# Inverse norms of queries and keys: one power on GpSimd in place of eleven VectorE instructions

## The chip, the cores and the metric

The kernel runs on one core of one Trainium2 chip. Its time is the device time of one execution in microseconds (us). The cores' engines are TensorE (PE in the profile; its weight loads are PEld), VectorE (DVE), ScalarE (ACT), GpSimd (POOL) and SyncE (SP, which here only issues transfers). Each engine runs its own instruction list in order, and the engines meet through semaphores.

## The reference, cut to what matters

The input is x of 4 x 1024 tokens with 128 channels, in float32. A linear attention with a layer norm comes first, and then six layers, each of a windowed attention and a feed-forward part. The change lies in the windowed attention:

```python
def l2norm(t):
    return t / jnp.maximum(jnp.linalg.norm(t, axis=-1, keepdims=True), 1e-12)

q = l2norm(q) * qs
k = l2norm(k) * ksc
...
sim = jnp.einsum('bhwie,bhwje->bhwij', bq, bk2) * QK_SCALE
sim = jnp.where(mask, -jnp.finfo(sim.dtype).max, sim)
attn = jax.nn.softmax(sim, -1)
```

There are 16 heads of 64 channels, so each token has 16 query norms and 16 key norms. What is wanted of each is the inverse square root of a sum of 64 squares, held above 1e-24.

## The kernel before, in words

Tokens lie on the 128 partitions, so 4096 tokens are 32 tiles, and six layers make 192 tiles of windowed attention. After the 32 tiles of a layer comes its feed-forward part in eight groups of four tiles. Every engine has a hand-written order of its own for one step, which works on several tiles at once, each in another stage of its way (the argument `s` of each helper is how many tiles back it works). `schedule` runs the steps two at a time in a loop. No planner orders anything: what an engine does next is the next line of its step. One period of this loop is one tile.

One tile goes through the engines like this. ScalarE copies the transposed tokens out of PSUM and makes their rounded upper part `xsT_hi`. VectorE subtracts to get the lower part `xsT_lo` (L974). TensorE projects the queries (L539 to L541, three products for each half). ScalarE squares them (L1351). VectorE multiplies the projection by the cosine and the sine table (`rotate`, L995), which frees the PSUM banks; TensorE then projects the keys into the same banks. VectorE sums the squares of queries and of keys per head (`sum_of_squares`, L1007) into `sumsq`, 128x32. GpSimd adds the two rotated parts (`add_rotated`, L1570 and L1571) into `qk_rot`.

The inverse norms come from `sumsq` by eleven VectorE instructions on 128x32: a clamp (L1022), a seed made on the bit pattern (L733), and three Newton rounds of three instructions (L737, L738, L739), each waiting for the one before through the semaphore `norm_step`. They are spread over VectorE's step: the calls `inverse_norms(i0, i1, s)` at L1069 to L1080 and L1100 to L1104 put one or two of them between other instructions. The result `rnorm` has three readers. GpSimd multiplies the rotated keys by it (`normalise_k`, L1580), and `k_rotated` then lets TensorE transpose them (L553). VectorE multiplies the row maxima of the scores by it (`softmax_bias`, L1058, to `nbias`). ScalarE takes it as the scale of the exponentials (L1365). VectorE also makes the reciprocals of the row sums (L984, `rrow`), by which GpSimd scales the probabilities (`normalise`, L1557).

GpSimd's step is: `normalise_k(1)`, `normalise(0, 2)`, `normalise(1, 2)`, `add_rotated("q", 0)`, `add_rotated("k", 0)`. TensorE's step starts with the transposes of the first half of the keys of two tiles back, and then the key projection of one tile back.

The functions that the change touches, and what calls them:

Of the kernel before, what the change touches and what calls it, by code (L numbers as in the profile page):

```python
# [54 lines left out]
RSQRT_OPS = 11  # L55
# [44 lines left out]
def build(nc, consts, at, x, Wq, bq, Wk, bk, Wv, bv, Wo, bo, Wqkv, q_scale, k_scale, Wout,  # L100
          ln_g, ln_b, W1, b1, W2, b2, out):
    ctx = ExitStack()
    with ctx:  # L103
# [3 lines left out]
        def sem(name):  # L107
            return ctx.enter_context(nc.semaphore(name))
# [55 lines left out]
        rs_t = sb("rs_t", [P, 2 * H])  # L164
        rs_h = sb("rs_h", [P, 2 * H])
# [80 lines left out]
        norm_step = sem("norm_step")  # L246
# [476 lines left out]
        def _(dve):  # L723
            v = nc.vector

            def rsqrt(y, src, t, h, first, steps, base):

                ops = [
                    first,
                    lambda: v.tensor_scalar(y.bitcast(I32), src.bitcast(I32), -0.5, RSQRT_MAGIC, ALU.mult, ALU.add),  # L733
                ]
                for _ in range(3):
                    ops += [
                        lambda: v.tensor_tensor(t, y, y, ALU.mult),  # L737
                        lambda: v.scalar_tensor_tensor(h, t, -0.5, src, ALU.mult, ALU.mult),  # L738
                        lambda: v.scalar_tensor_tensor(y, h, 1.5, y, ALU.add, ALU.mult),  # L739
                    ]  # L740
                assert len(ops) == RSQRT_OPS

                def op(i):
                    if i:
                        dve.wait_ge(steps, base + i)
                    ops[i]().then_inc(steps, 1)
                return op


# [159 lines left out]
            with dve.Fori(0, DEPTH) as l:  # L909
# [26 lines left out]
                def step(k, par, it):  # L936
# [65 lines left out]
                    def sum_of_squares(qk, s):  # L1002
                        if not there(k, it, s):
                            return
                        T, n = T0 - s, "qk".index(qk)
                        dve.wait_ge(squared[qk], done(T))
                        v.tensor_reduce(sumsq[:, n * H:(n + 1) * H],  # L1007
                                        heads(squares[:, n * INNER:(n + 1) * INNER]), AX,
                                        ALU.add).then_inc(summed[qk], 1)

                    def inverse_norms(i0, i1, s):

                        if not there(k, it, s):
                            return
                        T, a = T0 - s, (par - s) % 2
                        if i0 == 0:
                            dve.wait_ge(summed["q"], done(T))
                            dve.wait_ge(summed["k"], done(T))
                        if i0 <= 1 < i1:
                            dve.wait_ge(k_rotated, done(T - 2))  # L1020
                        op = rsqrt(rnorm[:, a, :], sumsq[:, :], rs_t[:, :], rs_h[:, :],
                                   lambda: v.tensor_scalar(sumsq[:, :], sumsq[:, :], 1e-24, None, ALU.max),  # L1022
                                   norm_step, RSQRT_OPS * T)
                        for i in range(i0, i1):
                            op(i)
# [24 lines left out]
                    def softmax_bias(half, s):  # L1050

                        if not there(k, it, s):
                            return
                        T, a, h = T0 - s, (par - s) % 2, slice(8 * half, 8 * half + 8)
                        dve.wait_ge(exp_done[half], done(T - 1))
                        dve.wait_ge(norm_step, RSQRT_OPS * T + RSQRT_OPS)
                        dve.wait_ge(max_done[half], done(T))
                        v.scalar_tensor_tensor(nbias[:, h], smax[:, h], -1.0, rnorm[:, a, h], ALU.mult,  # L1058
                                               ALU.mult).then_inc(bias_ready[half], 1)
# [9 lines left out]
                    inverse_norms(3, 4, 1)  # L1069
                    if it is not None or k != 1:  # L1070
                        xsT_lower(0)
                    inverse_norms(4, 5, 1)
                    maxima(1, 2)
                    inverse_norms(5, 6, 1)
                    residual(3)
                    inverse_norms(6, 8, 1)
                    softmax_bias(1, 2)
                    inverse_norms(8, 9, 1)
                    row_reciprocals(0, 2)
                    inverse_norms(9, 11, 1)  # L1080
# [17 lines left out]
                    sum_of_squares("k", 0)  # L1098
                    maxima(0, 1)
                    inverse_norms(0, 1, 0)  # L1100
                    softmax_bias(0, 1)
                    inverse_norms(1, 2, 0)
                    rotate("k", 0, 0)
                    inverse_norms(2, 3, 0)  # L1104
# [365 lines left out]
        def _(pool):  # L1470
            g = nc.gpsimd

            g.memset(x_tok[:, :], 0.0).then_inc(zeroed, 1)
# [71 lines left out]
            with pool.Fori(0, DEPTH) as l:  # L1545
                def step(k, par, it):
# [25 lines left out]

                    def normalise_k(s):
                        if not there(k, it, s):
                            return
                        T, a = T0 - s, (par - s) % 2
                        pool.wait_ge(added["k"], done(T))
                        pool.wait_ge(norm_step, RSQRT_OPS * T + RSQRT_OPS)
                        kk = heads(qk_rot[:, 1, :])
                        g.tensor_tensor(kk, kk, rnorm[:, a, H:2 * H].unsqueeze(2).broadcast_to([P, H, D]),  # L1580
                                        ALU.mult).then_inc(k_rotated, 1)

                    normalise_k(1)
# [185 lines left out]
```

## Time and profile before

| | |
|---|---|
| median of 3 runs | 4097.17 us (4088.42 to 4102.23) |
| profiled execution, span | 4091.2 us; its own time outside the span is not listed apart |
| PE busy | 3424.9 us (84%) |
| PEld busy | 2264.8 us (55%) |
| DVE busy | 3354.0 us (82%) |
| ACT busy | 3114.5 us (76%) |
| POOL busy | 2097.8 us (51%) |
| granted TensorE clock, mean | 0.931 |

The span goes from the first to the last instruction of the profiled execution. Busy shares are means over stages: in the 32 tiles of a layer's attention the engines are busier than in its feed-forward part. A timeline row gives start, duration, engine, line, what is written from what, and in brackets the idle time just before it with what ended it. Rows on one engine may overlap by about 0.1 us, since the end of one instruction lies beside the start of the next.

### The profile page before, as it was taken

Reading aid. Unit: us, or ns where it says so; the run is one execution under the profiler, and the core shown is the slowest. Engines: PE = TensorE matmul, PEld = TensorE weight load, DVE = VectorE, ACT = ScalarE, POOL = GpSimd, SP = SyncE. Lnnn points to the kernel's source line nnn. Section 1 sums busy time; section 2 is a strip of 40 time slices with the busy share of each in tenths; the row PEclk is TensorE's granted clock in tenths of the full one; section 3 lists DMA queues with packets and bytes.
Section 4 is the critical chain, followed back from the end, with each engine's and each line's share of the span. In section 5 each row is a group of like instructions: output and inputs, shape, how many; then the busy total and the mean of one; then the engine's idle time right before and its main releaser. Section 6 shows DMA issues by size and latency. Waiting matters only on the chain. (4 is left out here: it accounts for less than half of the span.)

```text
span 4091.2 us, 121860 instructions
## 1 busy us (share of the span) xinstructions
PE 3424.9 (84%) x40924; PEld 2264.8 (55%) x40924; DVE 3354.0 (82%) x6043; ACT 3114.5 (76%) x9641; POOL 2097.8 (51%) x2534
## 2 busy tenths in 40 slices
PE   5688987788989679988688888877899867988977
PEld 4455555655555555555465555555555545555555
DVE  7798997489999569999659989856899966999975
ACT  3488897378998459988638888846889954998883
POOL 3455554455555345555445555534555544555544
PEclk8799998899999889999889999988999988999998
DMA  2000000100000100000100000010000010000001
GB/s 61 10 4 4 4 4 25 27 6 4 4 4 3 43 12 4 4 4 4 31 21 5 4 4 4 2 43 11 4 4 4 4 36 17 4 4 4 4 24 42
DMA packets 109598, 51.94 MB, mean 13 GB/s; under 512 B 62726, under 2 KB 106628, under 8 KB 108420
## 3 DMA queue, kind: packets, MB, share of 16 engines
q1 hardware_dynamic: 109444, 49.99, 4.9%
q8 instruction: 84, 1.38, 0.1%
q14 instruction: 70, 0.57, 0.0%
HBM read 22.57 MB, written 2.10 MB: 6 GB/s over the span
## 5 line engine op out<-in xcount | busy, mean ns | idle before, releaser
L1365 ACT ACTIVATE probs<-s_ps,nbias,rnorm 128x64 f32<-128x64 f32 x3072 | 1209.2, 412 | 92.3 <-DVE nbias L1058 82.7
L1570 POOL TENSOR_TENSOR qk_rot<-by_cos,by_sin 128x512 f32<-128x512 f32 x384 | 487.7, 1270 | 629.1 <-DVE by_sin L995 629.1
L604 PE MATMUL ring<-wvo,xsT 128*32 128x512 f32 x6144 | 776.5, 625 | 1.5 <-ACT qT L1173 1.0
L1557 POOL TENSOR_TENSOR probs<-probs,rrow 128x256 f32<-128x256 f32 x768 | 454.5, 613 | 565.7 <-DVE rrow L984 565.7
L1365 ACT ACTIVATION_READ_ACCUMULATOR probs<-s_ps,nbias,rnorm 128x1 f32 x3072 | 649.5, 211 | 0.0
L539 PE MATMUL qk_ps<-wqk_hi,xsT_hi 128*128 128x512 f32 x756 | 342.9, 454 | 333.8 <-DVE xsT_lo L974 333.8
L1351 ACT ACTIVATE squares<-qk_ps 128x1024 f32<-128x1024 f32 x378 | 386.1, 1021 | 222.6 <-PE qk_ps L541 222.0
L1580 POOL TENSOR_TENSOR qk_rot<-qk_rot,rnorm 128x1024 f32<-128x1024 f32 x192 | 365.3, 1902 | 361.6 <-DVE rnorm L739 361.6
L1007 DVE TENSOR_REDUCE sumsq<-squares 128x16 f32<-128x1024 f32 x384 | 464.0, 1210 | 82.8 <-ACT squares L1351 82.8
L553 PEld LDWEIGHTS ring<-cst,qk_rot 128*128 128x128 f32 x3072 | 372.1, 147 | 286.1 <-issue 216.9
L995 DVE TENSOR_TENSOR by_cos<-qk_ps,rotary 128x1024 f32<-128x1024 f32 x378 | 460.5, 1218 | 84.4 <-ACT squares L1351 54.0
L553 PE MATMUL ring<-cst,qk_rot 128*128 128x128 f32 x3072 | 478.8, 289 | 44.8 <-POOL qk_rot L1580 33.4
L1571 POOL TENSOR_TENSOR qk_rot<-by_cos,by_sin 128x512 f32<-128x512 f32 x384 | 502.3, 1308 | 0.0
L995 DVE TENSOR_TENSOR by_sin<-qk_ps,rotary 128x1024 f32<-128x1024 f32 x378 | 458.5, 1213 | 0.0
L590 PE MATMUL s_ps<-kT,qT 128*32 128x128 f32 x12288 | 415.6, 276 | 0.0
L622 PE MATMUL ring<-vo,pT 128*32 128x128 f32 x12288 | 384.6, 278 | 5.0 <-ACT pT L1173 5.0
L539 PEld LDWEIGHTS qk_ps<-wqk_hi,xsT_hi 128*128 128x128 f32 x756 | 148.7, 197 | 422.0 <-issue 334.1
L590 PEld LDWEIGHTS s_ps<-kT,qT 128*32 128x32 f32 x12288 | 312.5, 110 | 121.1 <-issue 121.1
L1173 ACT ACTIVATE kT<-ring 64x512 f32<-64x512 f32 x576 | 340.3, 591 | 40.4 <-PE ring L553 33.5
L1173 ACT ACTIVATE vo<-ring 128x512 f32<-128x512 f32 x576 | 332.3, 608 | 34.5 <-PE ring L604 33.7
L604 PEld LDWEIGHTS ring<-wvo,xsT 128*32 128x32 f32 x6144 | 169.2, 114 | 333.2 <-issue 302.5
L622 PEld LDWEIGHTS ring<-vo,pT 128*32 128x32 f32 x12288 | 333.6, 112 | 28.3 <-issue 7.3
(166 smaller groups left out, 6427.7 us busy)
## 6 DMA issues: line engine op xcount, KB each, us to landing
xs<-x_tok SPq DMA_DIRECT2D x194, 64.0 KB, 1.9
qk_rot<-L_ffn_Wqkv SPq DMA_DIRECT2D x7, 1024.0 KB, 6.5
by_cos<-x_tok SPq DMA_DIRECT2D x48, 128.0 KB
by_cos<-x_tok SPq DMA_DIRECT2D x48, 127.0 KB
wv<-L_ffn_Wqkv SPq DMA_DIRECT2D x7, 512.0 KB, 8.4
wo_pad<-L_ffn_Wo SPq DMA_DIRECT2D x14, 256.0 KB, 7.7
x_keep<-L_attn_x SPq DMA_DIRECT2D x4, 512.0 KB, 4.9
out<-x_keep SPq DMA_DIRECT2D x4, 512.0 KB, 4.5
```

The costliest lines, as they stand in the source:

```text
L539: mm(half, xsT_hi[:, a, :], wqk_hi[:, cols], start=True, stop=False)
L553: last = nc.tensor.transpose(r[:, p * P:(p + 1) * P], qk_rot[:, 1 if qk == "k" else 0, c:c + P], ident)
L590: last = mm(s_ps[WIN * w:WIN * (w + 1), half, p * P:(p + 1) * P], qT[:, 4 * half + p, WIN * w:WIN * (w + 1)], kT[:, 4 * half + p, :, c:c + ...
L604: last = mm(r[WIN * mh:WIN * (mh + 1), :], xsT[:, a, WIN * w:WIN * (w + 1)], wvo[:, mh, :, :], start=True, stop=True)
L622: last = mm(r[WIN * w:WIN * (w + 1), 0:C], pT[:, quad, side, WIN * w:WIN * (w + 1)], vo[:, at_w, quad * C:(quad + 1) * C], start=(n == 0), ...
L995: last = v.tensor_tensor(heads((by_sin if part else by_cos)[:, n, :]), heads(projection_banks(qk, k, it, s)), rotary[2 * n + part][:, bass ...
L1007: v.tensor_reduce(sumsq[:, n * H:(n + 1) * H], heads(squares[:, n * INNER:(n + 1) * INNER]), AX, ALU.add).then_inc(summed[qk], 1)
L1173: return nc.scalar.activation(out_, in_, ACT.Copy)
L1365: last = nc.scalar.activation(probs[:, a, h // 4, :, h % 4, :], s_ps[:, half, c:c + 2 * WIN].rearrange("p (s c) -> p s c", s=2), ACT.Exp, ...
L1557: last = g.tensor_tensor(p, p, r, ALU.mult)
L1570: g.tensor_tensor(d[:, :, lo], cs[:, :, lo], sn[:, :, hi], ALU.add)
L1571: g.tensor_tensor(d[:, :, hi], cs[:, :, hi], sn[:, :, lo], ALU.add).then_inc(added[qk], 1)
```

## The change

`minus_half` is a column of -0.5, written once by GpSimd at the start. VectorE keeps the clamp, in one place, after the sum of the keys' squares. The seed and the three Newton rounds go. GpSimd raises `sumsq` to the power -0.5 in one instruction at the head of its step, ahead of `normalise_k`. `clamped` and `rnormed` take the place of `norm_step`. As before, the new writer of `rnorm` waits until the keys of two tiles back are normalised, and now it waits also until their exponentials are done; `sum_of_squares` waits until the power of the tile before has read `sumsq`.

```diff
         def _(dve):
-            def rsqrt(y, src, t, h, first, steps, base):
-                ops = [
-                    first,
-                    lambda: v.tensor_scalar(y.bitcast(I32), src.bitcast(I32), -0.5, RSQRT_MAGIC, ALU.mult, ALU.add),
-                ]
-                for _ in range(3):
-                    ops += [
-                        lambda: v.tensor_tensor(t, y, y, ALU.mult),
-                        lambda: v.scalar_tensor_tensor(h, t, -0.5, src, ALU.mult, ALU.mult),
-                        lambda: v.scalar_tensor_tensor(y, h, 1.5, y, ALU.add, ALU.mult),
-                    ]
...
                         T, n = T0 - s, "qk".index(qk)
+                        dve.wait_ge(rnormed, done(T - 1))
                         dve.wait_ge(squared[qk], done(T))
...
+                    def clamped_squares(s):
+                        if not there(k, it, s):
+                            return
+                        T = T0 - s
+                        dve.wait_ge(summed["q"], done(T))
+                        dve.wait_ge(summed["k"], done(T))
+                        v.tensor_scalar(sumsq[:, :], sumsq[:, :], 1e-24, None, ALU.max).then_inc(clamped, 1)
...
                         dve.wait_ge(exp_done[half], done(T - 1))
-                        dve.wait_ge(norm_step, RSQRT_OPS * T + RSQRT_OPS)
+                        dve.wait_ge(rnormed, done(T))
...
-                    inverse_norms(3, 4, 1)
                     if it is not None or k != 1:
                         xsT_lower(0)
-                    inverse_norms(4, 5, 1)
                     maxima(1, 2)
-                    inverse_norms(5, 6, 1)
                     residual(3)
-                    inverse_norms(6, 8, 1)
                     softmax_bias(1, 2)
-                    inverse_norms(8, 9, 1)
                     row_reciprocals(0, 2)
-                    inverse_norms(9, 11, 1)
                     rotate("q", 0, 0)
...
                     sum_of_squares("k", 0)
+                    clamped_squares(0)
                     maxima(0, 1)
-                    inverse_norms(0, 1, 0)
                     softmax_bias(0, 1)
-                    inverse_norms(1, 2, 0)
                     rotate("k", 0, 0)
-                    inverse_norms(2, 3, 0)
                     rotate("k", 1, 0)
...
+            g.memset(minus_half[:, :], -0.5)
             g.memset(x_tok[:, :], 0.0).then_inc(zeroed, 1)
...
+                    def inverse_norms(s):
+                        if not there(k, it, s):
+                            return
+                        T, a = T0 - s, (par - s) % 2
+                        for half in range(2):
+                            pool.wait_ge(exp_done[half], done(T - 2))
+                        pool.wait_ge(k_rotated, done(T - 2))
+                        pool.wait_ge(clamped, done(T))
+                        g.tensor_tensor(rnorm[:, a, :], sumsq[:, :], minus_half[:, :].broadcast_to([P, 2 * H]),
+                                        ALU.pow).then_inc(rnormed, 1)
...
                         pool.wait_ge(added["k"], done(T))
-                        pool.wait_ge(norm_step, RSQRT_OPS * T + RSQRT_OPS)
+                        pool.wait_ge(rnormed, done(T))
...
+                    inverse_norms(1)
                     normalise_k(1)
```

## Rows read from the trace of the kernel before

**Rows 1.** The page's first lines: span, and each engine's busy time.
```profile
span 4091.2 us, 121860 instructions
PE 3424.9 (84%) x40924; PEld 2264.8 (55%) x40924; DVE 3354.0 (82%) x6043; ACT 3114.5 (76%) x9641; POOL 2097.8 (51%) x2534
```

**Rows 2.** Busy time by window: stretch, length, PE, PEld, DVE, ACT, POOL, clock, DMA share.
```profile
407.50:424.00 16.50, 14.43 (x195) 9.35 (x191) 15.51 (x28) 14.44 (x49) 9.24 (x10) 0.94 0.01 4
424.00:441.50 17.50, 15.79 (x211) 9.57 (x207) 14.98 (x27) 15.08 (x49) 9.20 (x9) 0.96 0.01 4
```

**Rows 3.** VectorE's timeline, 403 to 421 us: start, duration, instruction, idle before.
```profile
403.05 1.16 DVE L974 TENSOR_TENSOR xsT_lo<-xsT,xsT_hi 128x128 fp32r<-128x128 f32 x1 [0.32 <-ACT xsT_hi L1173]
404.12 1.27 DVE L739 SCALAR_TENSOR_TENSOR rnorm<-rs_h,rnorm 128x32 f32<-128x32 f32 x1
...
407.62 1.22 DVE L995 TENSOR_TENSOR by_cos<-qk_ps,rotary 128x1024 f32<-128x1024 f32 x1 [0.24 <-issue]
...
412.82 0.18 DVE L984 RECIPROCAL rrow<-psum_row 128x8 f32<-128x8 f32 x1
...
415.46 1.31 DVE L1058 SCALAR_TENSOR_TENSOR nbias<-smax,rnorm 128x8 f32<-128x8 f32 x1
416.69 0.17 DVE L733 TENSOR_SCALAR rnorm<-sumsq 128x32 int32<-128x32 int32 x1
416.77 1.21 DVE L995 TENSOR_TENSOR by_cos<-qk_ps,rotary 128x1024 f32<-128x1024 f32 x1
417.91 0.18 DVE L737 TENSOR_TENSOR rs_t<-rnorm 128x32 f32<-128x32 f32 x1
418.01 1.21 DVE L995 TENSOR_TENSOR by_sin<-qk_ps,rotary 128x1024 f32<-128x1024 f32 x1
...
419.72 1.07 DVE L974 TENSOR_TENSOR xsT_lo<-xsT,xsT_hi 128x128 fp32r<-128x128 f32 x1 [0.40 <-ACT xsT_hi L1173]
```

**Rows 4.** GpSimd's timeline over the same stretch.
```profile
404.01 1.33 POOL L1571 TENSOR_TENSOR qk_rot<-by_cos,by_sin 128x512 f32<-128x512 f32 x1
407.47 1.90 POOL L1580 TENSOR_TENSOR qk_rot<-qk_rot,rnorm 128x1024 f32<-128x1024 f32 x1 [2.12 <-DVE rnorm L739]
...
413.09 1.18 POOL L1557 TENSOR_TENSOR probs<-probs,rrow 128x256 f32<-128x256 f32 x2 [2.58 <-DVE rrow L984]
...
415.47 1.27 POOL L1571 TENSOR_TENSOR qk_rot<-by_cos,by_sin 128x512 f32<-128x512 f32 x1
419.39 1.25 POOL L1570 TENSOR_TENSOR qk_rot<-by_cos,by_sin 128x512 f32<-128x512 f32 x1 [2.65 <-DVE by_sin L995]
```

**Rows 5.** ScalarE's timeline over the same stretch.
```profile
406.03 1.02 ACT L1351 ACTIVATE squares<-qk_ps 128x1024 f32<-128x1024 f32 x1 [0.92 <-PE qk_ps L541]
...
419.31 0.31 ACT L1173 ACTIVATE xsT_hi<-xsT 128x128 fp32r<-128x128 f32 x1
```

**Rows 6.** TensorE's timeline: second half of query, first half of key transposes.
```profile
409.01 1.13 PE L553 MATMUL ring<-cst,qk_rot 128*128 128x128 f32 x8
```

**Rows 7.** VectorE's timeline in a tile with a shorter period.
```profile
1186.67 0.15 DVE L1058 SCALAR_TENSOR_TENSOR nbias<-smax,rnorm 128x8 f32<-128x8 f32 x1
...
1194.68 1.23 DVE L995 TENSOR_TENSOR by_cos<-qk_ps,rotary 128x1024 f32<-128x1024 f32 x1 [0.24 <-issue]
```

**Rows 8.** ScalarE's timeline in the same tile.
```profile
1192.55 1.02 ACT L1351 ACTIVATE squares<-qk_ps 128x1024 f32<-128x1024 f32 x1
```

**Rows 9.** Waits over the whole span: total us, times, longest us.
```profile
PE ring L553 <- POOL qk_rot L1580: 33.4, 37, 4.0
DVE by_cos L995 <- issue: 30.4, 129, 0.2
```

**Rows 10.** Groups by line: count, busy us, mean ns, idle before and releaser.
```profile
L739 DVE SCALAR_TENSOR_TENSOR rnorm<-rs_h,rnorm 128x32 f32<-128x32 f32 x576 | 304.9, 529 | 13.5
L1580 POOL TENSOR_TENSOR qk_rot<-qk_rot,rnorm 128x1024 f32<-128x1024 f32 x192 | 365.3, 1902 | 361.6 <-DVE rnorm L739 361.6
L1480 POOL TENSOR_TENSOR ln_rs<-ln_rs 128x4 f32<-128x4 f32 x156 | 30.5, 198 | 276.2 <-DVE ln_rs L766 269.1
```

More of the change, by code:

```diff
@@ L54 @@
 RSQRT_MAGIC = 1597463007.0
-RSQRT_OPS = 11
 NEWTON_OPS = 12
@@ L163, in build @@
         sumsq = sb("sumsq", [P, 2 * H])
-        rs_t = sb("rs_t", [P, 2 * H])
-        rs_h = sb("rs_h", [P, 2 * H])
+        minus_half = sb("minus_half", [P, 1])
         rnorm = sb("rnorm", [P, 2, 2 * H])
@@ L245, in build @@
             {qk: tile_sem(f"{qk}_{n}") for qk in "qk"} for n in ("projected", "squared", "summed", "read", "added")]
-        norm_step = sem("norm_step")
+        clamped, rnormed = tile_sem("clamped"), tile_sem("rnormed")
         k_rotated = tile_sem("k_rotated")
@@ L724, in _ @@
             v = nc.vector
-            def rsqrt(y, src, t, h, first, steps, base):
-                ops = [
-                    first,
-                    lambda: v.tensor_scalar(y.bitcast(I32), src.bitcast(I32), -0.5, RSQRT_MAGIC, ALU.mult, ALU.add),
-                ]
-                for _ in range(3):
-                    ops += [
-                        lambda: v.tensor_tensor(t, y, y, ALU.mult),
-                        lambda: v.scalar_tensor_tensor(h, t, -0.5, src, ALU.mult, ALU.mult),
-                        lambda: v.scalar_tensor_tensor(y, h, 1.5, y, ALU.add, ALU.mult),
-                    ]
[L741 to L747, printed above, removed]
             def wide(ap):
@@ L1009, in sum_of_squares @@
                                         ALU.add).then_inc(summed[qk], 1)
-                    def inverse_norms(i0, i1, s):
+                    def clamped_squares(s):
                         if not there(k, it, s):
                             return
[L1015 to L1025, printed above, removed]
+                        T = T0 - s
+                        dve.wait_ge(summed["q"], done(T))
+                        dve.wait_ge(summed["k"], done(T))
+                        v.tensor_scalar(sumsq[:, :], sumsq[:, :], 1e-24, None, ALU.max).then_inc(clamped, 1)
                     def carry(s):
```

## The prediction

> **What bounds the kernel now.** I read the page's busy line first, then the busy time by window over single tiles of the attention, then the four timelines side by side, and last the list of waits. The page shows four engines between 51% and 84% over a span of 4091.2 us [rows 1], so no engine is the bound by its share alone. Inside a tile the picture is tighter: in a period of 16.5 us VectorE works 15.5, TensorE and ScalarE 14.4, GpSimd 9.2; in the next period of 17.5 us TensorE works 15.8 and VectorE 15.0 [rows 2]. Idle time is left on every engine, so a loop of dependences sets the period, not a queue that is full. The timelines show the loop, here from one start of `rotate("q")` to the next:
>
> - VectorE from the cosine product of the queries at 407.62 to the reciprocals `rrow` at 412.82: 5.2 us [rows 3].
> - GpSimd scales the probabilities from 413.09 and adds the rotated queries until 416.74 [rows 4]. VectorE's `nbias` (L1058), which reads two SBUF tensors, is recorded from 415.46 for 1.31 us and ends just behind that instruction of GpSimd [rows 3, 4]: 3.95 us from the reciprocals.
> - ScalarE makes four exponentials and then `xsT_hi`, done at 419.62 [rows 5]: 2.85 us.
> - VectorE makes `xsT_lo`, from 419.72 to 420.79. It ends behind GpSimd's first addition of the keys, 419.39 to 420.64 [rows 3, 4]: 1.17 us.
> - TensorE projects the queries and ScalarE squares them: from the end of `xsT_lo` at 404.21 to the end of the square at 407.05 are 2.84 us [rows 3, 5], and the next cosine product follows 0.57 us later.
>
> These are 5.2 + 3.95 + 2.85 + 1.17 + 2.84 + 0.57 = 16.6 us, the period. Beside it TensorE has a path of its own: after the query projection it goes on without a pause to the first key transposes, done at 410.14 [rows 6], and projects the keys.
>
> **The change, part by part.** The sum is made on the span, 4091.2 us, which lies 6.0 us under the median of the runs, 4097.2; the time outside the span stays.
>
> *Removed between the two parts of `rotate("k")`.* The seed moves the cosine product from 416.69 to 416.77 and the first Newton instruction the sine product from 417.91 to 418.01 [rows 3]: 0.18 us. The sine product releases GpSimd's addition of the keys, and the end of that addition's first part releases `xsT_lo`. So 0.18 us comes off the loop in each tile: 192 x 0.18 = 35 us.
>
> *Removed between `xsT_lo` and `rotate("q")`.* Eight Newton instructions go. One of them (L739, from 404.12) is held for 1.27 us behind GpSimd's second addition, which ends at 405.34 [rows 3, 4]; that is why L739 has a mean of 529 ns over 576 instructions [rows 10]. VectorE reaches the cosine product late in 129 tiles, those where the releaser is "issue" and not the square [rows 9]. Where the square is the releaser the start follows it by 0.26 us (I take this lag for all), so 407.62 could be 407.31: 0.31 us. In the tile with the shorter period the square ends at 1193.57 [rows 8] and the product starts at 1194.68 [rows 7] and not at 1193.83: 0.85 us. By the gaps between `xsT_lo` and the product about 80 of the 129 are of the first kind and 49 of the second: 80 x 0.31 + 49 x 0.85 = 66 us. The other tiles gain nothing here.
>
> *Not removed.* The held `nbias` of the first half stays: it waits for a GpSimd instruction that is still there. `softmax_bias(1, 2)` loses the eight instructions before it and now queues behind GpSimd's second addition in place of L739; nobody on the loop waits for it, since `rotate("q")` waits for the square 1.7 us longer (407.05 against 405.34). The clamp stays, one place earlier; that costs nothing, since `maxima` behind it is delayed by what the clamp no longer takes afterwards.
>
> *Added on GpSimd.* One power on 128x32 between the addition of the keys and `normalise_k`. No row shows a power, and its duration, X, decides this case. From below: a GpSimd instruction on 128x4 takes 198 ns [rows 10]. Two instructions of one kind give the cost of a pass over the elements: 1.90 us for 1024 and 1.18 / 2 = 0.59 us for 256 [rows 4], so 1.7 ns an element and 0.15 us fixed, or 0.2 us for 32 elements. [...] If it took a hundred such passes it would be 0.15 + 100 x 32 x 0.0017 = 5.6 us; with 25 passes, a polynomial each way, 1.5 us. I take 1.5 us, nearest to the measured rows with some arithmetic per element, and keep 0.2 and 5.6 as ends.
>
> *What hides it.* GpSimd now idles 2.12 us before `normalise_k`, waiting for the last Newton instruction [rows 4], 361.6 us in all [rows 10]. The power takes that place: it needs only the clamp, done long before. The addition of the keys ends at 405.34, 0.18 us earlier after the change, so `k_rotated` comes at 405.16 + X + 1.90, plus 0.1 for the hand-over. TensorE comes to the first key transposes at about 409.57, half way through the row of eight [rows 6]. So X up to 2.4 us costs nothing in this tile. Behind `normalise_k` GpSimd has 2.58 us of idle time before `rrow` of the second half [rows 4], so its own queue is not the bound for X below some 4.5 us. In the tiles with the shorter period there is less cover: TensorE already waits for `normalise_k` in 37 places, 33.4 us in all [rows 9], so the 0.85 us counted there won't all arrive. Queued behind the power are `normalise_k` and both probability scalings; VectorE's added wait in `sum_of_squares` for the power of the tile before is met some 5 us ahead.
>
> *Where rule and row meet.* The row first: two-input VectorE instructions that start while a GpSimd instruction runs end when it ends (L739 and L1058 above, 1.27 and 1.31 us in place of 0.2) [rows 3, 4]. The Trainium skill, GPSIMD Engine Reference, section Key points, says the same of the cause: GpSimd shares its SBUF interfaces with VectorE instructions that have two SBUF inputs. By that rule a long power would also hold `softmax_bias(1, 2)` if it came too late for the gap before it; in the sum it slips in ahead and costs nothing.
>
> *Sum.* 35 + 66 = 101 us if all arrives. I take off a quarter for TensorE's own path (kept busy until 410.14 with the product's end at 409.97, so almost level): 76 us. 4097 - 76 is about 4020 us.
>
> **The rivals.**
>
> *The power is long.* For X above 2.4 us `k_rotated` is late for TensorE, and with it the key projection, the key copies on VectorE, and the reciprocals behind them. Each tile then loses X - 2.4 and gains about 0.4. At X = 4: 192 x 1.2 = 230 us, 4330 us. At X = 5.6: 192 x 2.8 = 540 us, 4635 us. It decides from X = 2.8 us. For it: nothing in the trace limits a power from above, and the layer norms of this kernel spend twelve GpSimd instructions of about 0.2 us on their own inverse roots. Against: only 32 elements a partition. The Trainium skill (GPSIMD Engine Reference, Performance pitfalls for Q7 kernels) has a rule on this side: a chain of dependent float32 operations costs 4 cycles an element for each link. By it, as an estimate, 25 links would be 100 cycles an element, 2.7 us for 32 elements at the page's 1.2 GHz, and the time about 4110 us. No row here shows it.
>
> *The gain is eaten.* TensorE's path is level with the loop, so the freed VectorE time turns into waits for it: 4085 to 4109 us.
>
> *The held `nbias` slips in.* In the tile with the shorter period `nbias` took 0.15 us because it came in ahead of GpSimd's second addition of the queries [rows 7]; the two start within 0.01 us of each other. It is a race in time, and every shift of VectorE's order moves it. If it were won in all of some 140 tiles in which it is lost now, 140 x 1.1 = 154 us more would go: about 3870 us. If it were lost everywhere, 50 x 1.1 = 55 us of the gain would go.
>
> **How the numbers follow.** A short power with the gain as summed: 0.46, its own range 3940 to 4085 us. Short, with the race mostly won: 0.09. Gain eaten: 0.08. Long power: 0.37, of which half below X = 4.3 us. A difference under 0.3%, 12 us, is no change here. So faster 0.55, same 0.08, slower 0.37. The range runs from 3890 (a part of the race won) to 4390 us (X of 4.3: 192 x 1.5 = 290).
>
> **What would show it.** The mean of the power on GpSimd: below 2.4 us the forecast stands, above 2.8 it falls. The waits: the "issue" wait of the cosine product should go and become one for the square; TensorE's wait for `qk_rot` from GpSimd should stay near 33 us, and grow with a long power. `xsT_lo` should end 0.18 us earlier behind `nbias`. The share of `nbias` instructions of more than 1 us, now some 140 in the first half, tells the race. The prediction is wrong if the power is longer than the hole it goes into, or if the race flips.

## The result, and the profile after

The changed kernel takes 4822.41 us (median of 4 runs, 4794.02 to 4831.69) against 4097.7 us: a ratio of 1.1757, with an interval of 1.1713 to 1.1801. The forecast was 4020 us, in a range of 3890 to 4390, so the time lies outside it and on the other side.

The page of the changed kernel, its busy line and four of its groups (line, engine, operation, output and inputs with shapes, count; busy us, mean ns; idle before and releaser):

```profile
span 4829.8 us, 118707 instructions
PE 3573.7 (74%) x40924; PEld 2437.3 (50%) x40924; DVE 2894.7 (60%) x4123; ACT 3129.0 (65%) x9641; POOL 3132.2 (65%) x2727
...
L551 PE MATMUL ring<-cst,qk_rot 128*128 128x128 f32 x3072 | 569.2, 317 | 648.2 <-POOL qk_rot L1552 637.4
L1542 POOL TENSOR_TENSOR rnorm<-sumsq,minus_half 128x32 f32<-128x32 f32 x192 | 1041.6, 5425 | 0.0
...
L914 DVE COPY kT<-ring 64x512 f32<-64x512 f32 x192 | 131.2, 683 | 706.3 <-PE ring L551 706.3
...
L1552 POOL TENSOR_TENSOR qk_rot<-qk_rot,rnorm 128x1024 f32<-128x1024 f32 x192 | 365.0, 1901 | 27.5
```

VectorE did become lighter: 2894.7 us of work where it had 3354.0 [rows 1]. The power takes 5425 ns. The normalisation of the keys (L1552), which used to wait 361.6 us for the last Newton instruction [rows 10], now follows the power at once, and the wait has moved one engine further: TensorE waits 637.4 us for it, where it waited 33.4 [rows 9], and VectorE waits 706.3 us for TensorE.

One tile after, 20.5 us long. First GpSimd, then TensorE, then VectorE, from their timelines (start, duration, instruction, idle before with its end):

```profile
450.48 1.25 POOL L1531 TENSOR_TENSOR qk_rot<-by_cos,by_sin 128x512 f32<-128x512 f32 x1 [3.48 <-DVE by_sin L969]
451.69 1.33 POOL L1532 TENSOR_TENSOR qk_rot<-by_cos,by_sin 128x512 f32<-128x512 f32 x1
452.99 5.43 POOL L1542 TENSOR_TENSOR rnorm<-sumsq,minus_half 128x32 f32<-128x32 f32 x1
458.56 1.90 POOL L1552 TENSOR_TENSOR qk_rot<-qk_rot,rnorm 128x1024 f32<-128x1024 f32 x1
```

```profile
456.70 0.66 PE L551 MATMUL ring<-cst,qk_rot 128*128 128x128 f32 x4
460.60 1.09 PE L551 MATMUL ring<-cst,qk_rot 128*128 128x128 f32 x4 [3.24 <-POOL qk_rot L1552]
461.34 0.78 PE L537 MATMUL qk_ps<-wqk_hi,xsT_hi 128*128 128x512 f32 x1
461.92 0.63 PE L538 MATMUL qk_ps<-wqk_lo,xsT_hi 128*128 128x512 f32 x1
```

```profile
454.94 1.23 DVE L969 TENSOR_TENSOR by_cos<-qk_ps,rotary 128x1024 f32<-128x1024 f32 x1 [1.77 <-ACT squares L1311]
...
457.81 0.68 DVE L1006 TENSOR_TENSOR kT<-kT,cst 128x512 f32<-128x512 f32 x1
461.82 0.68 DVE L914 COPY kT<-ring 64x512 f32<-64x512 f32 x1 [3.33 <-PE ring L551]
```

From the end of the addition to the start of the normalisation are 5.54 us. TensorE has nothing else to do for 3.24 of them. When it starts again, its four key transposes take 1.09 us where the four before the wait took 0.66, and the product L538 0.63 where it took 0.39 in the query projection of the same tile. The busy time by window around the wait (length, PE, PEld, DVE, ACT, POOL, then the granted clock, DMA share and GB/s):

```profile
452.00:460.00 8.00, 5.36 (x38) 2.60 (x38) 4.72 (x8) 5.68 (x19) 7.86 (x3) 1.00 0.00 0
460.50:463.20 2.70, 2.60 (x9) 2.24 (x10) 1.38 (x2) 1.36 (x5) 1.10 (x2) 0.50 0.00 0
```

So the granted clock fell behind the idle time, from 1.00 to 0.50, that is from the upper of its two levels, 2.4 GHz, to the lower, 1.2. VectorE's key copy waits for that too, and with it the sums, the reciprocals and the next turn of the loop. The cosine product of the queries, on the other hand, now waits for the square and not for VectorE, as forecast.

### The profile page after: what moved, and what is told of

It is laid out like the page before. It is cut to its first block and busy times, and to the rows that moved or that the text cites. A ratio compares the mean times of both kernels' runs of the same rounds, so it can differ in the third digit from the quotient of the medians.

```text
span 4829.8 us, 118707 instructions
## 1 busy us (share of the span) xinstructions
PE 3573.7 (74%) x40924; PEld 2437.3 (50%) x40924; DVE 2894.7 (60%) x4123; ACT 3129.0 (65%) x9641; POOL 3132.2 (65%) x2727
## 5 line engine op out<-in xcount | busy, mean ns | idle before, releaser
L551 PE MATMUL ring<-cst,qk_rot 128*128 128x128 f32 x3072 | 569.2, 317 | 648.2 <-POOL qk_rot L1552 637.4
L1542 POOL TENSOR_TENSOR rnorm<-sumsq,minus_half 128x32 f32<-128x32 f32 x192 | 1041.6, 5425 | 0.0
L551 PEld LDWEIGHTS ring<-cst,qk_rot 128*128 128x128 f32 x3072 | 415.8, 161 | 912.5 <-issue 848.3
L602 PE MATMUL ring<-wvo,xsT 128*32 128x512 f32 x6144 | 748.3, 605 | 0.0
L537 PE MATMUL qk_ps<-wqk_hi,xsT_hi 128*128 128x512 f32 x756 | 426.8, 565 | 322.9 <-DVE xsT_lo L948 310.2
L914 DVE COPY kT<-ring 64x512 f32<-64x512 f32 x192 | 131.2, 683 | 706.3 <-PE ring L551 706.3
L537 PEld LDWEIGHTS qk_ps<-wqk_hi,xsT_hi 128*128 128x128 f32 x756 | 194.5, 257 | 395.7 <-issue 330.4
L1552 POOL TENSOR_TENSOR qk_rot<-qk_rot,rnorm 128x1024 f32<-128x1024 f32 x192 | 365.0, 1901 | 27.5
L538 PE MATMUL qk_ps<-wqk_lo,xsT_hi 128*128 128x512 f32 x756 | 371.0, 491 | 0.0
```

The costliest lines, as they stand in the source:

```text
L537: mm(half, xsT_hi[:, a, :], wqk_hi[:, cols], start=True, stop=False)
L551: last = nc.tensor.transpose(r[:, p * P:(p + 1) * P], qk_rot[:, 1 if qk == "k" else 0, c:c + P], ident)
L602: last = mm(r[WIN * mh:WIN * (mh + 1), :], xsT[:, a, WIN * w:WIN * (w + 1)], wvo[:, mh, :, :], start=True, stop=True)
L1542: g.tensor_tensor(rnorm[:, a, :], sumsq[:, :], minus_half[:, :].broadcast_to([P, 2 * H]), ALU.pow).then_inc(rnormed, 1)
```

## The experiments

Times are medians; each ratio is to the kernel before on the same chip, with its interval. Four chips were used: one for the first three experiments and the power in two halves, a second for the two and four microseconds, Newton's rounds and the clock in the kernel before, a third for the whole power between the additions and for the last experiment, a fourth for the multiplications between the additions. The kernel before has medians of 4097, 4105, 4082 and 4063 us on them, so microseconds of different chips compare to some 40 us at best.

**A short instruction in place of the power.**

```diff
-                                        ALU.pow).then_inc(rnormed, 1)
+                                        ALU.subtract).then_inc(rnormed, 1)
```

> The changed kernel with one operation name altered: the power becomes a subtraction on the same 128x32, so the inverse norms are left out and everything else (order, waits, clamp, what VectorE no longer does) stays. Theory A: all of the loss is the time that the power stands in front of the keys' normalisation, and what TensorE's clock does in the wait it makes. Then this kernel shows the rest of the forecast: the instruction takes about 0.25 us, TensorE's wait for GpSimd's keys falls from 637 us to under 60, and the time is 4020 us (3940 to 4085), below the kernel before. Rival B: the new waits and the undivided clamp (mean 0.93 us now, 0.36 before) cost by themselves; then it stays above 4100 us.

Measured: 3999.03 us, ratio 0.9744 (0.9695 to 0.9794). GpSimd's instruction and the tile around it, on VectorE and GpSimd:

```profile
455.95 0.24 POOL L1542 TENSOR_TENSOR rnorm<-sumsq,minus_half 128x32 f32<-128x32 f32 x1
456.34 1.90 POOL L1552 TENSOR_TENSOR qk_rot<-qk_rot,rnorm 128x1024 f32<-128x1024 f32 x1
```

```profile
453.88 0.97 DVE L948 TENSOR_TENSOR xsT_lo<-xsT,xsT_hi 128x128 fp32r<-128x128 f32 x1 [0.60 <-ACT xsT_hi L1133]
...
457.91 1.23 DVE L969 TENSOR_TENSOR by_cos<-qk_ps,rotary 128x1024 f32<-128x1024 f32 x1 [1.77 <-ACT squares L1311]
```

From the end of `xsT_lo` to the cosine product are 3.06 us, where they were 3.41 [rows 3]: the forecast had 3.10. TensorE waits for GpSimd's keys 18.1 us in all. The new waits and the undivided clamp cost nothing that shows, rival B falls, and the whole loss of the change lies in the power's duration.

**The same duration without a power.** Three multiplications on 128x960 into a scratch tile, each waiting for the one before, and then the short subtraction.

```diff
...
+                        for i in range(3):
+                            pool.wait_ge(filled, passed(3 * T + i))
+                            g.tensor_tensor(scratch[:, 0:960], const("rotary")[:, 0:960],
+                                            minus_half[:, :].broadcast_to([P, 960]), ALU.mult).then_inc(filled, 1)
```

> The power replaced by three multiplications on 128x960 into a scratch tile and one subtraction on 128x32, together about 5.5 us of GpSimd time in the same place; the inverse norms are left out. Theory A: only the duration counts, so the time is that of the changed kernel, 4822 us, within 60. Rival C: the power hurts by its nature, as one long instruction that VectorE's two-input instructions can't pass; then four shorter ones between which they can slip in give clearly less, 4700 us or below.

Measured: 4864.38 us, ratio 1.1857 (1.1796 to 1.1918), 42 us above the changed kernel. The filling turned out longer than the power: from the addition to the normalisation are 6.0 us in the mean, against 5.5. TensorE's wait for the keys is 711.3 us. In the place ahead of the keys' normalisation a duration is what counts, whatever fills it.

**TensorE kept busy in its wait.**

```diff
                         r = bank(f"{qk}T{half}", s)
+                        if qk == "k" and half == 0:
+                            for n in range(24):
+                                nc.tensor.transpose(r[:, (n % 4) * P:(n % 4 + 1) * P], ident, ident)
                         pe.wait_ge(k_rotated if qk == "k" else added["q"], done(T))
```

> The changed kernel, with 24 transposes of the identity on TensorE ahead of its wait for the normalised keys, into the bank that the key transposes then overwrite; about 3.4 us of work where it now waits 3.25 us. Theory A with the clock as a part of it: after the wait the four key transposes take 1.09 us where they took 0.60, and the first five key products 0.63 where they took 0.39; kept busy, TensorE does them at full clock and each tile is about 1.4 us shorter: 192 x 1.4 = 270 us, 4550 us (4480 to 4640). Rival D: the clock after the wait doesn't matter, because the loop goes another way; then 4820 us, or more where the filling delays the key transposes.

Measured: 4578.31 us, ratio 1.1158 (1.1102 to 1.1215). TensorE's timeline, with the added transposes in L550:

```profile
456.59 2.78 PE L550 MATMUL ring<-cst 128*128 128x128 f32 x24
459.92 0.66 PE L554 MATMUL ring<-cst,qk_rot 128*128 128x128 f32 x4 [0.55 <-POOL qk_rot L1555]
460.34 0.48 PE L537 MATMUL qk_ps<-wqk_hi,xsT_hi 128*128 128x512 f32 x1
460.65 0.40 PE L538 MATMUL qk_ps<-wqk_lo,xsT_hi 128*128 128x512 f32 x1
```

The power is as long as before and the keys are as late, but the transposes take 0.66 and not 1.09 us, and L538 0.40 and not 0.63. The mean granted clock of the run is 0.954, against 0.892. The clock's part of the loss is 4822 - 4578 = 244 us, 1.3 us a tile. The Trainium skill, Perfetto Trace Analysis, section Matmul Optimizations, advises that matmuls run back to back in batches, since the engine scales its power with its use; these two runs agree, and the 244 us are what it is worth here.

**Two and four microseconds in the same place.** The same multiplications, one (with no wait behind it) and two of them.

> The changed kernel with the power replaced by one multiplication on 128x960 (1.79 us) and the short subtraction on 128x32 (0.24 us), 2.0 us together; the inverse norms are left out. The prediction's cover was 2.4 us. If it is right, this costs nothing against the kernel with the short subtraction alone: 3999 us, within 20. If the cover is really under 1 us, each tile loses 1 us and more: 4190 us or above.

> The same with two multiplications on 128x960, some 4.0 us in front of the keys' normalisation. The kernel with three of them, 5.8 us, took 4864 us, the one with none 3999. Theory A with the cover of 2.4 us and a clock that falls only where TensorE waits long: 192 x (4.0 - 2.4) = 307 us and up to 1.4 us a tile for the clock, so 4300 us if the clock stays up and 4570 if it falls in each tile; I expect 4400. A straight line through the two known points would give 4620 us: (4.0 - 0.24) / 5.6 x 865 + 3999 = 4580.

Measured: 4041.47 us (ratio 0.9854, 0.9809 to 0.9899) with one, 4286.39 us (1.0451, 1.0402 to 1.0499) with two. GpSimd and TensorE with two:

```profile
449.10 3.64 POOL L1546 TENSOR_TENSOR scratch<-cst,minus_half 128x960 f32<-128x960 f32 x2
452.70 0.24 POOL L1548 TENSOR_TENSOR rnorm<-sumsq,minus_half 128x32 f32<-128x32 f32 x1
453.08 1.90 POOL L1558 TENSOR_TENSOR qk_rot<-qk_rot,rnorm 128x1024 f32<-128x1024 f32 x1
```

```profile
455.13 0.63 PE L553 MATMUL ring<-cst,qk_rot 128*128 128x128 f32 x4 [1.67 <-POOL qk_rot L1558]
455.51 0.48 PE L539 MATMUL qk_ps<-wqk_hi,xsT_hi 128*128 128x512 f32 x1
```

3.98 us stand in front of the normalisation and TensorE idles 1.67: the cover is 2.3 us. In the changed kernel it is 5.57 - 3.24 = 2.3 as well. The forecast had 2.4. With 2.0 us the loss over the shortest is 42 us, more than the 20 I allowed, between two chips. TensorE's waits for the keys grow by only 15 us of it (33.4 against 18.1). Of the 44 us between the two traces 17 lie in the 168 tiles inside the layers and 27 in the rest, beside the feed-forward parts; their cause stays open. With two multiplications TensorE's clock stays up behind 1.67 us (0.63 us for the four transposes); with the power it falls behind 3.24. So the time is not a straight line: with 0.3, 2.1, 4.0 and 6.0 us in the mean between the addition and the normalisation it is 3999, 4041, 4286 and 4864 us. The last 2.1 us cost 578 us, of which the delay alone is some 192 x 2.1 = 400.

**The power in two halves.** The keys' half between the two additions, the queries' half behind the normalisation of the keys.

```diff
...
-                    inverse_norms(1)
                     normalise_k(1)
+                    inverse_norms("q", 1)
                     normalise(0, 2)
                     normalise(1, 2)
                     add_rotated("q", 0)
+                    inverse_norms("k", 0)
                     add_rotated("k", 0)
```

> The full computation with the power cut in two of 128x16: the keys' half between the two additions, where GpSimd idles 2.65 us before and 3.5 us after the change, and the queries' half behind the normalisation of the keys. If the duration goes with the elements (5.43 us for 32, so 2.7 us for 16), the keys' half fits its hole, TensorE's wait for the keys falls back to some 30 us, and GpSimd is busy 14.6 of 16 us. Theory A: 4000 to 4120 us, near the kernel before. If the power has a large fixed part, two of them cost more than one and the time stays above 4400 us. If the order costs more through held two-input instructions of VectorE, xsT_lo above all, 4150 to 4300 us.

Measured: 4177.85 us, ratio 1.0182 (1.0130 to 1.0234). The group, and the tile on GpSimd and VectorE:

```profile
L1545 POOL TENSOR_TENSOR rnorm<-sumsq,minus_half 128x16 f32<-128x16 f32 x384 | 1116.9, 2909 | 14.2 <-DVE sumsq L994 14.2
```

```profile
450.82 2.91 POOL L1545 TENSOR_TENSOR rnorm<-sumsq,minus_half 128x16 f32<-128x16 f32 x1
453.69 1.26 POOL L1532 TENSOR_TENSOR qk_rot<-by_cos,by_sin 128x512 f32<-128x512 f32 x1
```

```profile
453.85 1.25 DVE L949 TENSOR_TENSOR xsT_lo<-xsT,xsT_hi 128x128 fp32r<-128x128 f32 x1 [0.69 <-ACT xsT_hi L1134]
```

If the duration goes in a straight line with the elements, a power costs (5425 - 2909) / 16 = 157 ns an element and some 0.4 us fixed. The long wait is gone, and the addition, which now starts 0.16 us ahead of `xsT_lo`, holds it nearly for its full length: a mean of 1243 ns, against 929 in the kernel before and 911 with the short subtraction.

The number is that of the third expectation, but the held instruction is the smaller part of it. `xsT_lo` now ends so late that TensorE waits 1.9 us for it in every tile, where it waited 1.5 with the short subtraction. In 86 of the 168 tiles inside the layers its clock falls behind this wait:

```profile
471.63 0.47 PE L538 MATMUL qk_ps<-wqk_hi,xsT_hi 128*128 128x512 f32 x1 [1.91 <-DVE xsT_lo L949]
...
472.44 0.63 PE L538 MATMUL qk_ps<-wqk_hi,xsT_hi 128*128 128x512 f32 x1
```

The tiles in which it stays up are 16.4 us long, those in which it falls 17.7. Over the kernel with the short subtraction the hold is worth (1.243 - 0.911) x 192 = 64 us and the clock, by these tiles, some 104, of 179 in all. No run here separates the two.

**The whole power between the additions.**

> The full computation with the whole power on 128x32 moved from the head of GpSimd's step to between its two additions, where it idles 2.5 us. Nothing else changes. TensorE's long wait for the keys should go (5.6 us of power, 2.5 idle there and 2.3 of cover behind it), but the second addition starts some 3 us later, and xsT_lo, a two-input instruction of VectorE that is then ready, is held until the power ends: about 2 us on the loop. I expect a period near 18 us: 4097 + 192 x 1.5 = 4380 us (4280 to 4480), clearly below the changed kernel's 4822 and above the 4178 of the split power. If a held xsT_lo is not on the loop, 4100 us.

Measured: 4090.59 us, ratio 1.0022 (0.9997 to 1.0047): not told from the kernel before. I had missed by 290 us. GpSimd, then VectorE:

```profile
446.38 5.43 POOL L1542 TENSOR_TENSOR rnorm<-sumsq,minus_half 128x32 f32<-128x32 f32 x1
451.77 1.28 POOL L1531 TENSOR_TENSOR qk_rot<-by_cos,by_sin 128x512 f32<-128x512 f32 x1
```

```profile
449.40 0.29 DVE L948 TENSOR_TENSOR xsT_lo<-xsT,xsT_hi 128x128 fp32r<-128x128 f32 x1 [0.70 <-ACT xsT_hi L1133]
...
450.43 0.17 DVE L1026 SCALAR_TENSOR_TENSOR nbias<-smax,rnorm 128x8 f32<-128x8 f32 x1
```

Both two-input instructions ran in the middle of the power, unhindered; `xsT_lo` has a mean of 312 ns here and 929 in the kernel before. The keys are still late, though less than in the changed kernel: TensorE waits 215.6 us for them in all (637.4 in the changed kernel, 33.4 in the one before). That is some 1 us a tile, and its clock stays up behind it:

```profile
456.42 0.63 PE L551 MATMUL ring<-cst,qk_rot 128*128 128x128 f32 x4 [0.93 <-POOL qk_rot L1552]
```

So this kernel equals the one before because a gain and a loss cancel: its tiles inside the layers take 16.4 us, against 16.0 with the short subtraction. That `xsT_lo` passed called for a test.

**Multiplications between the additions.** The kernel above, with the three multiplications and the subtraction of the second experiment in place of the power.

> The kernel with the whole power between the two additions, the power replaced by three multiplications on 128x960 and the short subtraction, about 5.8 us in the same place; the inverse norms are left out. In the kernel with the power there, xsT_lo started in the middle of the power and took 0.29 us, and the time was 4091 us, not 4380 as I had expected. Theory P: a power, unlike an addition or a multiplication of GpSimd, lets VectorE's two-input instructions pass while it runs. Then xsT_lo is held here, by up to 1.8 us, its mean is above 0.8 us, and each tile loses about that: 4200 us or more. Rival: whatever runs there, xsT_lo passes, because it comes at a lucky moment; then its mean stays near 0.3 us and the time is that of the power's kernel plus 0.3 us a tile, 4100 to 4150.

Measured: 4159.35 us, ratio 1.0207 (1.0133 to 1.0281). The two groups of `xsT_lo`, first with the power and then with the multiplications:

```profile
L948 DVE TENSOR_TENSOR xsT_lo<-xsT,xsT_hi 128x128 fp32r<-128x128 f32 x192 | 59.9, 312 | 165.8 <-ACT xsT_hi L1133 165.8
```

```profile
L950 DVE TENSOR_TENSOR xsT_lo<-xsT,xsT_hi 128x128 fp32r<-128x128 f32 x192 | 154.3, 804 | 169.2 <-ACT xsT_hi L1135 169.2
```

A mean of 804 against 312 ns: the multiplications hold it and the power does not. The mean is at the bound I set; the time, 69 us above, lies between the two forecasts, and the two ratios' intervals don't overlap. `nbias` went from 318 to 731 ns, too. Whether it is the operation that lets them pass, or that a power works on 32 elements in 5.4 us and the multiplications on 960 in 1.8, no run here separates.

**Newton's rounds on GpSimd.** No power: VectorE keeps the clamp (and halves) and the seed; GpSimd makes twelve short instructions on 128x32, eight between the additions and four ahead of the keys' normalisation.

```diff
...
+                        ops = [(t, y, y, ALU.mult), (t, t, sumsq[:, :], ALU.mult), (t, three, t, ALU.subtract),
+                               (y, y, t, ALU.mult)] * 3
...
+                    inverse_norms(8, 12, 1)
                     normalise_k(1)
...
                     add_rotated("q", 0)
+                    inverse_norms(0, 8, 0)
                     add_rotated("k", 0)
```

> The full computation without the power: VectorE keeps the clamp (which now halves too) and the seed, GpSimd makes the three Newton rounds in twelve short instructions on 128x32, eight of them between the two additions, where it idles 2.5 us, and four ahead of the keys' normalisation, where up to 2.4 us are covered. At 0.25 us each these are 2.0 and 1.0 us, so both fit. Theory A (it is duration in front of the keys, and held two-input instructions of VectorE behind late additions): within 60 of the kernel with the short subtraction, 4000 to 4060 us, faster than the kernel before. Rival: a short GpSimd instruction that waits for the one before takes more than 0.3 us, the eight push the keys' addition and with it xsT_lo, and it is 4100 us or more.

Measured: 4034.71 us, ratio 0.9836 (0.9790 to 0.9881), the fastest full computation here, below both kernels. One of four groups of such instructions:

```profile
L1560 POOL TENSOR_TENSOR rs_t<-rs_t,sumsq 128x32 f32<-128x32 f32 x576 | 147.8, 257 | 45.1
```

With the wait between them they start every 0.32 us, so the four at the head take 1.3 us (cover 2.3) and the eight 2.5 us, in a hole of 2.5.

The trace has a second thing to teach. VectorE's seed, which reads one SBUF tensor only, now starts while GpSimd's second addition of the queries runs, and is held until it ends; `nbias` behind it is not. VectorE twice, then GpSimd:

```profile
455.77 0.71 DVE L1005 TENSOR_SCALAR rnorm<-sumsq 128x32 int32<-128x32 int32 x1
456.40 0.15 DVE L1039 SCALAR_TENSOR_TENSOR nbias<-smax,rnorm 128x8 f32<-128x8 f32 x1
```

```profile
455.17 1.27 POOL L1546 TENSOR_TENSOR qk_rot<-by_cos,by_sin 128x512 f32<-128x512 f32 x1
```

So it is not only instructions with two SBUF inputs that are held: the seed has a mean of 680 ns, and took 0.17 where it started as the addition ended [rows 3].

**TensorE's clock in the kernel before.** Eight transposes of the identity ahead of the wait for `xsT_lo`.

```diff
+                        if it is not None and qk == "q" and n == 0:
+                            pe.wait_ge(read["k"], done(T - 1))
+                            for m in range(8):
+                                nc.tensor.transpose(qk_ps[:, (m % 4) * P:(m % 4 + 1) * P], ident, ident)
                         pe.wait_ge(xsT_hi_ready, done(T))
```

> The kernel before, with eight transposes of the identity on TensorE ahead of its wait for xsT_lo in the query projection (into the bank that the projection then overwrites), in the loop's steps; about 1 us of the 1.7 to 2.1 us that it idles there. It asks what part of the gain of the kernel with the short subtraction is TensorE's clock and what part VectorE's path. If the 17.5 us tiles come from a clock that falls behind that idle time, they become 16.5: 44 tiles by about 1.1 us, 4050 us. If VectorE's path makes the period, it stays at 4097 within 12; in the tiles with little idle time the transposes may delay the projection by up to 0.6 us.

Measured: 4047.03 us, ratio 0.9866 (0.9820 to 0.9912). Busy time by window (PE, PEld, DVE, ACT, POOL, then the granted clock), first the kernel before, then this one, then the one with the short subtraction:

```profile
300.00:600.00 300.00, 268.17 (x3564) 168.17 (x3555) 272.39 (x496) 265.18 (x862) 166.40 (x162) 0.97 0.01 4
```

```profile
300.00:600.00 300.00, 286.32 (x3770) 184.40 (x3771) 277.82 (x509) 269.65 (x882) 170.58 (x166) 1.00 0.01 4
```

```profile
300.00:600.00 300.00, 267.20 (x3745) 172.16 (x3744) 233.77 (x329) 275.20 (x902) 175.72 (x186) 1.00 0.01 4
```

The clock goes from 0.97 to 1.00 in this stretch, and some 50 us go. In the kernel before it falls in the longer tiles, such as the second of [rows 2]:

```profile
420.89 0.47 PE L539 MATMUL qk_ps<-wqk_hi,xsT_hi 128*128 128x512 f32 x1 [2.07 <-DVE xsT_lo L974]
...
422.12 0.62 PE L541 MATMUL qk_ps<-wqk_hi,xsT_lo 128*128 128x512 f32 x1
422.54 1.05 PE L553 MATMUL ring<-cst,qk_rot 128*128 128x128 f32 x4
```

Taken from the end of one `xsT_lo` to the next, 45 tiles inside the layers have a mean of 17.5 us in the kernel before and of 16.45 with the eight transposes. With the short subtraction the clock is 1.00 too, without added work, and TensorE waits 1.5 us for `xsT_lo` in each tile: a part of the gain of 98 us there is the clock, which the forecast had not counted.

**Both together.** The Newton rounds on GpSimd with the eight transposes.

> The kernel with the Newton rounds on GpSimd, and the eight transposes on TensorE ahead of the query projection beside it. Those transposes gave the kernel before 1.3%, through the clock. Here the products of the query projection already stand at 0.39 us in the tiles looked at, so if that gain was only the clock, there is nothing left: 4035 us within 15. If it was something else (the order in which the projection's waits are met), another 40 us go.

Measured: 4045.47 us, ratio 0.9916 (0.9888 to 0.9944). Nothing more is gained (the kernel without the transposes took 4035 us on another chip, and the two profiled executions 4041 and 4039 us), so in the kernel before the transposes worked through the clock alone, as far as these runs tell.

## Why the prediction was wrong, step by step

- *Added on GpSimd* is the step that failed. X, the duration of the power, was taken as 1.5 us and is 5.43. It lay within the stated ends of 0.2 and 5.6, but the value was set "nearest to the measured rows", and no measured row said anything of the work a power does per element: 157 ns against the 1.7 ns of a pass. It is as if ninety passes had been made, near the hundred that I had put as the far end; the 25 passes behind the 1.5 us have no row or run behind them, and no run shows what a power is made of. With the ends as far apart as that, and the outcome changing sign between them, the range should have reached to the price of the upper end.
- *The long power*, the rival with 0.37, is what happened, with its mechanism: past a cover of 2.3 us (2.4 forecast) TensorE, the key copies and the reciprocals are late one after the other. Its price was short: at 5.43 us it gives 4097 + 192 x (5.43 - 2.8) = 4602 us. That is within 24 us of the 4578 measured with TensorE kept busy. The missing term is the clock, 244 us, which falls in a wait of 3.24 us and not in one of 1.67. The estimate from the rule of the Trainium skill (GPSIMD Engine Reference, Performance pitfalls for Q7 kernels), 25 dependent links at 4 cycles each, gave 2.7 us, half of the 5.43 measured. The time that I put beside it, 4110 us, was also wrong: by the rival's own terms 2.7 us give 4097 - 192 x 0.1 = 4078.
- *What bounds the kernel* held for the tiles of 16.5 us. The tile of 17.5 us beside it was left unexplained: in it TensorE's clock is down for a part of the time, as the experiment with the eight transposes showed, and the sum has no term for that.
- *Removed on VectorE* held in part, and its total is near by luck. 4020 us were forecast for a short power, and with a short instruction it is 3999. Inside the layers of the kernel before, 93 tiles have a mean of 16.5 us, 45 of 17.5 and 32 of 15.2; with the short subtraction the same tiles have 16.0, 16.1 and 16.0. In the 93 the sum was right: 0.46 us went, where 0.18 + 0.31 were forecast. The short tiles were to lose a further 0.85 us, and instead grew by 0.8, which cost 26 us. (They are also fewer than counted: of the late cosine products some 90 are late by about 0.3 us more than the lag and 35 by about 0.8, where the prediction has 80 and 49.) The 45 long ones gave 61 us, and with nothing but the eight transposes they gave 46: this is the clock, which the sum put at nothing. Two of the signs came as forecast: the "issue" wait of the cosine product became one for the square, and `xsT_lo` ends 0.18 us earlier behind `nbias` (3.84 us after its end and not 4.02).
- *The held `nbias`*: the race did flip, the other way than the rival that was priced highest. In the kernel before `nbias` of the first half takes more than 1 us in 142 of 198 places; in all 32 short tiles it slipped in ahead of the addition. With the short subtraction none takes more than 1 us, which by the stated sign would be a race won, but in nearly all (180) it starts later, takes 0.49 us and still ends with GpSimd's addition (450.52 to 451.01, the addition until 450.99). The short tiles are gone, and the 26 us above are its price, where the prediction had 55 for a race lost everywhere. With Newton's rounds on GpSimd `nbias` slips by, but the seed ahead of it is held instead, and nothing is won.
- *Where rule and row meet*: the rule that the Trainium skill states (GPSIMD Engine Reference, Key points), on the SBUF interfaces shared with VectorE instructions of two SBUF inputs, agrees with the rows for additions and multiplications (1.25 us and a mean of 804 ns for `xsT_lo`). For the power the measurement says otherwise (312 ns), and I had also used the rule to expect 4380 us of the kernel with the power between the additions, which took 4091.

## What to carry to other kernels

An operation that no trace of the kernel shows needs its own measurement before its place is argued: here its duration decided between a ratio of 0.974 and one of 1.176. A sum that comes near is not yet a sum that is right: the rest of this one came within 21 us with a gain by the clock missing on one side and a lost race on the other. Read the clock tile by tile before you take a longer tile for a longer loop. Measure the cover too, since it is what a new instruction may cost for nothing, and remember that beyond it the price isn't linear: a wait long enough for TensorE's clock to fall is paid twice, once in the wait and once behind it. If a slow instruction must stay, put it where its engine idles and others don't wait: the same power moved four lines down took 4091 us and not 4822.

## What the runs showed of the hardware that was not expected

- A power on GpSimd took 5425 ns on 128x32 and 2909 ns on 128x16: 157 ns an element between the two, against 240 ns for a subtraction on all of 128x32.
- While a power runs, VectorE's two-input instructions pass (`xsT_lo` 0.29 us in the middle of one, mean 312 ns); while multiplications or additions run, they are held (mean 804 ns in the same place).
- GpSimd's additions also hold VectorE instructions with one SBUF input: the seed 0.71 us where it took 0.17, and the clamp of the changed kernel 1.02 us (from 446.01, beside an addition that ends at 447.00), with a mean of 928 ns against 363 before.
- TensorE's clock stayed up behind waits of 1.5 us in all 168 tiles inside the layers with the short subtraction, fell in 86 of 168 behind waits of 1.9 us with the power in two halves, and fell in 39 of 50 such tiles behind waits of 2.1 us in the kernel before. Behind 3.24 us in the changed kernel it was down, and filling that wait with transposes gave 244 us.
